# Second stage of a fused transformer kernel: who writes the rows of negated maxima

## The chip, the cores and the metric

The kernel runs on one core of one Trainium2 chip. The metric is the time on the device in microseconds; lower is better. Three runs of the kernel before took 1945.25, 1947.76 and 1950.1 us, so the median is 1947.76 us.

## The reference

The input x is (4, 256, 512) and the context is (4, 1601, 512), all in float32. Four blocks follow one another, each adding to x what it computes of layernorm(x):

```
x = x + L0_xattn(layernorm(x), ctx)   # latent cross attention, 16 heads, 1601 keys
x = x + L0_ffn(layernorm(x))          # int4 weights, dequantised by groups of 128
x = x + L1_xattn(layernorm(x), ctx)   # grouped attention, 16 heads on 4 key heads, 256 + 1601 keys
x = x + L1_ffn(layernorm(x))          # a dense layer plus a mixture of low-rank experts
```

The change is in the first block:

```
C_q = Q @ Wq_d;  C_kv = K @ Wkv_d
scores = einsum('bnhl,bkl->bhnk', (C_q @ W_qk).reshape(b, n, H, LKV), C_kv) / sqrt(LKV)
attn = softmax(scores, axis=-1)
out = einsum('bhnk,bkhd->bnhd', attn, (C_kv @ Wv_u).reshape(b, nkv, H, HD))
```

## The kernel before, in words

The kernel has three stages. The first turns the context and multiplies it with the key and value weights. The second (`latent_attention_and_ffn`) does the first attention and the dequantised layer. The third (`grouped_attention`) does the rest. Each engine runs its own list of instructions in a written order, and semaphores join them.

The second stage goes through 16 groups s (4 batches by 4 groups of 4 heads). A group has 1024 queries, which lie along the free axis, and 13 tiles of keys. For each tile TensorE multiplies keys with queries (`scores`, L952, two halves of 512 columns), ScalarE takes the exponential (L1080), and TensorE multiplies the result with the values (`values`, L965).

The softmax needs the maximum of every query before its scores are exponentiated. So a group's maxima are found one group ahead: TensorE computes 32 tiles of plain scores with the queries on the partitions (L1020), VectorE reduces each along the keys (L1187) and folds the 32 columns into `mx`, 128 x 8 (L1193). TensorE transposes `mx` into 8 rows of 128 in PSUM (L1023). From them `shift_rows` (L124) writes 8 rows of 1024 below the queries in `ast`: row j holds the negated maxima of its own 128 queries and zeros elsewhere, as a product of the 8 transposed rows, repeated eight times, with the small diagonal `negid`, repeated along its 128 columns. The keys have rows of ones beside them, so that the scores of L952 come out with the maximum subtracted. The product that makes the 8 rows of group s is called row s here; row 16 belongs to the third stage's first group and goes to `home[1]`.

All small products (maxima, rows, the raising of a finished group's output, queries, keys and values of the third stage) share a ring of four PSUM banks. Product n waits until product n - 4 has been read (`read`, L851). `course(s)` (L800) writes down the order of a group's work for all engines. Near its end stand: the values of tiles 10 and 11; row s + 1; three maxima of group s + 2; the values of tile 12; then the `tail`, which for groups 4 to 13 holds products of the other layers (an `ffn` pair, or one or two of `q`); then three more maxima. Then the next group's scores begin, and the first of them waits for `row_done` (L946). Groups 0 to 3, 14 and 15 have no tail.

GpSimd has little to do in this stage: a few memsets at its start, and nine times the inverse square root of a layernorm (`pool_root`, L87), each a chain of 14 small instructions, which starts when VectorE has the statistics and on which VectorE waits later.

Of the kernel before, what the change touches and what calls it, by code (L numbers as in the profile page):

```python
# [13 lines left out]
P = 128  # L14
BANK = 512
B, T, D = 4, 256, 512
# [7 lines left out]
H1, KV1, HD1 = 16, 4, 96  # L24
S1 = float(HD1) ** -0.5
G = 4
NG = H0 // G
GC = G * T
QT = GC // P
# [57 lines left out]
def pool_root(pool, chain, mv, v, t, y):  # L87

    chain.link(pool.tensor_scalar(v[:, :], mv[:, :, 1], EPS, None, ALU.add))  # L89
    chain.link(pool.tensor_scalar(y[:, :].bitcast(I32), v[:, :].bitcast(I32), -0.5, RSQRT_GUESS, ALU.mult, ALU.add))  # L90
    for i in range(3):
        chain.link(pool.tensor_tensor(t[:, :], y[:, :], y[:, :], ALU.mult))
        chain.link(pool.tensor_tensor(t[:, :], t[:, :], v[:, :], ALU.mult))
        chain.link(pool.tensor_scalar(t[:, :], t[:, :], -0.5, 1.5, ALU.mult, ALU.add))
        last = pool.tensor_tensor(y[:, :], y[:, :], t[:, :], ALU.mult)
        if i < 2:
            chain.link(last)
    return last
# [23 lines left out]
def shift_rows(dve, rows, turned, negid):  # L122

    return dve.tensor_tensor(rows.rearrange("p (j m) -> p j m", j=QT),  # L124
                             turned.rearrange("p (o m) -> p o m", o=1).broadcast_to([QT, QT, P]),
                             negid[:, :].rearrange("p (j o) -> p j o", o=1).broadcast_to([QT, QT, P]), ALU.mult)
# [562 lines left out]
def latent_attention_and_ffn(nc, A, ident, negid, ps, ln, home, wkvh, wkvl, wqh, wql, w0T, bias0, wqd, wqk, wvu, cq,  # L689
# [7 lines left out]
    S = B * NG  # L697
# [14 lines left out]
    with ExitStack() as ctx:  # L712
        def sb(name, shape, dt=F32):
            return ctx.enter_context(nc.sbuf_tensor(name, shape, dt))

        def sem(name):
            return ctx.enter_context(nc.semaphore(name))
# [9 lines left out]
        ast = sb("ast", [HD1 + QT, H0 * T], F32R)  # L727
        pr = sb("pr", [P, NPR, GC])
        osb = sb("osb", [P, BANK])
        pm = sb("pm", [P, QT, len(cuts)])  # L730
        mx = sb("mx", [P, QT])
        rec = sb("rec", [P, TT * G])
        tmp = sb("tmp", [P, TT, G * HD0])
        qst = sb("qst", [P, 2, 2, BANK])
# [4 lines left out]
        xa_done, xn_done = sem("xa_ready"), sem("xn_ready")  # L739
        k0_in, q0_in = [sem("k0_in0"), sem("k0_in1")], [sem("q0_in0"), sem("q0_in1")]  # L740
        ahi, xth_done, qhi = sem("a_hi"), sem("xt_hi"), sem("q_hi")
        mxr_done, row_done = sem("max_ready"), sem("max_row")
        s_mm, exp_done, av_mm, o_done = sem("scores"), sem("probs"), sem("values"), sem("o_copied")
        product = sem("ring_product")
        done = {"act": sem("ring_read_by_act"), "dve": sem("ring_read_by_dve")}
# [3 lines left out]
        stats_done, root_done = sem("norm_stats"), sem("norm_root")  # L749
# [83 lines left out]
        def last_reader(g):  # L833
            if g[0] in ("xat", "cq") or g[0] == "xt" and g[2:] == (0, 0):
                return "act"
            return "dve"

        at, order, count = {}, [], {"act": 0, "dve": 0}
# [5 lines left out]
        def bank_of(g):  # L844
            return bank(M0 + at[g][0] % RB)

        def turned(g):

            return product, at[g][0] + 1

        def read(g):  # L851

            return (row_done, g[1] + 1) if g[0] == "row" else (done[last_reader(g)], at[g][1])

        def qkv_free(e, u):

# [2 lines left out]
        def width(u):  # L859
            return WK if u >= NQ + NKL else T if u == NQ + NKL - 1 else 2 * T  # L860
# [65 lines left out]
        @block.gpsimd  # L926
        def _(pool):
            ready = Chain(pool, const, 0)
            for i in range(2):
                ready.link(pool.memset(cst[i][0:HD1, NC:NC + 1].bitcast(F32), 0.0))  # L930
            ready.link(pool.memset(home[0][0:HD1, NK:NK + 1].bitcast(F32), 0.0))
            ready.link(pool.memset(home[0][HD1:HD1 + QT, :].bitcast(F32), 1.0))
            ready.link(pool.memset(cst[1][HD1:HD1 + QT, :].bitcast(F32), 1.0))
            ready.link(pool.memset(cv[:, :, :, HD0:64], 0.0))
            ready.link(pool.memset(cv[:, :, :, HD0:HD0 + 1], 1.0))
            roots = Chain(pool, step_r, 0)
            for n in range(3 * (B - 1)):
                pool.wait_ge(stats_done, n + 1)
                pool_root(pool, roots, ln["mv"], ln["v"], ln["t"], ln["y"]).then_inc(root_done, 1)

        @block.tensor
        def _(pe):
# [56 lines left out]
            def ring_item(g):  # L999
                n, out = at[g][0], bank_of(g)  # L1000
                if n >= RB:
                    pe.wait_ge(*read(order[n - RB]))
# [121 lines left out]
        def _(dve):  # L1124
# [8 lines left out]
            norms, waiting = [0], []  # L1133
# [11 lines left out]
            def normalise_xa(f):  # L1145
                dve.wait_ge(xa_in, 16 * f)
                begin_norm(xa, xa, chain_a, xa_done)

            def normalise(e, k):
                if e < B - 1:  # L1150
                    begin_norm(x[:, e % 2, :, :], xn, chain, xn_done)
                else:
                    layernorm(dve, chain, xn, x[:, e % 2, :, :], ln["st"], ln["mv"], ln["v"], ln["t"], ln["u"], ln["y"])\
                        .then_inc(xn_done, 1)
# [22 lines left out]
            def ring_item(g):  # L1177
                if last_reader(g) == "act":
                    return
                src = bank_of(g)  # L1180
                if g[0] == "max":
                    _, s, i = g
                    if i == 0 and s:
                        dve.wait_ge(mxr_done, s)
                    dve.wait_ge(*turned(g))
                    j, ch = divmod(i, len(cuts))
                    dve.reduce_max(pm[:, j, ch:ch + 1], src[:, 0:(cuts if s < S else next_cuts)[ch][1]], AX)\  # L1187
                        .then_inc(done["dve"], 1)
                    if i == NI - 1:
                        dve.wait_ge(*read(g))  # L1190
                        if s:
                            dve.wait_ge(*turned(("row", s - 1)))
                        dve.reduce_max(mx[:, :], pm[:, :, :], AX).then_inc(mxr_done, 1)  # L1193
                elif g[0] == "row":
                    grp = g[1] % NG
                    dve.wait_ge(*turned(g))
                    rows = ast[HD1:HD1 + QT, grp * GC:(grp + 1) * GC] if g[1] < S \
                        else home[1][HD1:HD1 + QT, 0:GC]
                    shift_rows(dve, rows, src[0:QT, 0:P], negid).then_inc(row_done, 1)
                elif g[0] == "raise":  # L1200
                    dve.wait_ge(*turned(g))
                    attended(g[1], src)
                    b, grp = divmod(g[1], NG)
                    if grp == NG - 1:
                        normalise(b, 0)
                    if grp == 1 and b + 1 < B:
                        normalise_xa(b + 1)
                elif g[0] == "a":
                    lo = ast[2 * HD0:3 * HD0, g[2] * BANK:(g[2] + 1) * BANK]
                    dve.wait_ge(ahi, 8 * g[1] + g[2] + 1)  # L1210
                    dve.tensor_tensor(lo, src[2 * HD0:3 * HD0, :], lo, ALU.subtract).then_inc(done["dve"], 1)
                elif g[0] == "xt":
                    cols = slice(2 * g[3], 2 * g[3] + 2)
                    if g[2] == 0:
                        dve.wait_ge(*turned(g))
                        dve.tensor_copy(xT[:, cols, :], src.rearrange("p (c m) -> p c m", c=2)).then_inc(done["dve"], 1)
                    else:
                        dve.wait_ge(xth_done, 2 * g[1] + g[3] + 1)
                        dve.tensor_tensor(xtl[:, cols, :], src.rearrange("p (c m) -> p c m", c=2), xth[:, cols, :],
                                          ALU.subtract).then_inc(done["dve"], 1)  # L1220
                elif g[0] == "ffn":
                    _, e, t = g
                    xs = x[:, e % 2, t, :]
                    dve.wait_ge(*turned(g))
                    dve.tensor_tensor(xs, src, xs, ALU.add).then_inc(done["dve"], 1)
                    dve.wait_ge(*read(g))
                    chain.link(dve.tensor_tensor(xs, xs, bias0[:, :], ALU.add))
                    if t == TT - 1:
                        normalise(e, 1)
                else:  # L1230
                    _, e, u = g
                    n = width(u)
                    dve.wait_ge(qhi, NU * e + u + 1)
                    dve.tensor_tensor(qst[:, u % 2, 1, 0:n].bitcast(F32R), src[:, 0:n], qst[:, u % 2, 0, 0:n], ALU.subtract)\
                        .then_inc(done["dve"], 1)
# [663 lines left out]
```

## Time and profile before

| what | value |
|---|---|
| median of three runs | 1947.76 us |
| profiled execution, its own time | 1948.22 us |
| its span, first to last instruction | 1946.4 us |
| TensorE busy | 1872.9 us, 96% |
| VectorE busy | 1019.9 us, 52% |
| ScalarE busy | 904.3 us, 46% |
| GpSimd busy | 655.7 us, 34% |
| mean granted TensorE clock | 0.967 of full speed |

Times in the rows are from the start of the span. PE is TensorE's matrix multiplication, PEld its loading of weights (the left operand), which overlaps the multiplication before it; DVE is VectorE, ACT ScalarE, POOL GpSimd. A bracket shows how long the engine sat idle before the first instruction of the row and who released it. In a timeline, like instructions that follow each other are merged, with their count behind x.

### The profile page before, as it was taken

How to read it: one execution, taken by the hardware profiler on the slowest of the kernel's cores; microseconds unless marked ns; L12 is line 12 of the kernel's file. 1: busy time of each engine (PE TensorE's matmuls, PEld its weight loads, DVE VectorE, ACT ScalarE, POOL GpSimd, SP SyncE). 2: the span in 40 equal slices, each digit the busy share in tenths (PEclk: the TensorE clock that was granted, in tenths of full speed). 3: DMA queues.
4: the chain of work that ended last, by engine and by line, in shares of the span. 5: the costliest groups of instructions: out<-in, count | busy, mean ns of one | idle time of the engine just before them, and what ended most of it. 6: DMA issues, size and time to landing. Idle time of an engine off the chain costs nothing. (4 is left out here: it accounts for less than half of the span.)

```text
span 1946.4 us, 23155 instructions
## 1 busy us (share of the span) xinstructions
PE 1872.9 (96%) x8570; PEld 1337.1 (69%) x8570; DVE 1019.9 (52%) x1852; ACT 904.3 (46%) x1726; POOL 655.7 (34%) x630
## 2 busy tenths in 40 slices
PE   7999997999999999999979999999999999999998
PEld 6999894444465555555577777767777677777764
DVE  3464434667655565665635555554444645554415
ACT  2333331445334344444326666645666456655660
POOL 0000000000000000000017777755777577766770
PEclk9999996899999999999989999999999999999998
DMA  5978863000010111021058444544444355443201
GB/s 182 286 243 268 280 209 113 1 1 18 29 59 27 34 66 33 33 67 44 22 177 197 111 108 118 133 124 116 126 113 112 81 132 135 124 124 98 69 25 44
DMA packets 192950, 208.42 MB, mean 107 GB/s; under 512 B 87425, under 2 KB 157569, under 8 KB 192838
## 3 DMA queue, kind: packets, MB, share of 16 engines
q1 hardware_dynamic: 177124, 188.92, 34.1%
q10 hardware_dynamic: 15714, 18.03, 3.1%
q8 instruction: 68, 1.11, 0.2%
q14 instruction: 44, 0.36, 0.1%
HBM read 128.90 MB, written 77.94 MB: 106 GB/s over the span
## 5 line engine op out<-in xcount | busy, mean ns | idle before, releaser
L1475 POOL TENSOR_TENSOR pl<-pf,ph 128x512 fp32r<-128x512 f32 (+1 forms) x480 | 623.4, 1320 | 258.6 <-ACT pf L1669 258.6
L1666 ACT ACTIVATE ph<-ps 128x512 fp32r<-128x512 f32 (+1 forms) x480 | 288.4, 601 | 361.9 <-PE ps L1562 361.9
L1749 DVE TENSOR_REDUCE pm<-ps 128x1 f32<-128x464 f32 x480 | 307.7, 642 | 249.5 <-PE ps L1493 245.9
L1187 DVE TENSOR_REDUCE pm<-ps 128x1 f32<-128x400 f32 (+3 forms) x544 | 283.1, 572 | 96.9 <-PE ps L1020 84.0
L1080 ACT ACTIVATE pr<-ps 128x512 f32<-128x512 f32 (+1 forms) x416 | 219.1, 601 | 193.9 <-PE ps L952 192.9
L1669 ACT ACTIVATE pf<-ps 128x512 f32<-128x512 f32 (+1 forms) x480 | 289.7, 603 | 0.7 <-POOL pl L1475 0.7
L965 PE MATMUL ps<-pr,cv 128*64 128x512 f32 (+1 forms) x832 | 209.0, 618 | 0.0
L1580 PE MATMUL ps<-ph,vh 128*97 128x512 f32 (+1 forms) x480 | 193.0, 402 | 0.0
L1583 PE MATMUL ps<-pl,vh 128*97 128x512 f32 (+1 forms) x480 | 190.1, 396 | 0.8 <-POOL pl L1475 0.7
L1581 PE MATMUL ps<-ph,vl 128*97 128x512 f32 (+1 forms) x480 | 189.9, 396 | 0.0
L89 POOL TENSOR_SCALAR ln_v<-ln_mv 128x2 f32<-128x2 f32 x9 | 1.9, 214 | 507.1 <-DVE ln_mv L70 507.1
L1493 PE MATMUL ps<-kh,qh 96*128 96x464 f32 x320 | 121.3, 379 | 5.6 <-DVE pm L1749 5.6
L1560 PE MATMUL ps<-qh,kh 104*128 104x512 f32 x300 | 121.7, 406 | 0.0
L965 PEld LDWEIGHTS ps<-pr,cv 128*64 128x64 f32 (+1 forms) x832 | 51.9, 139 | 88.1 <-issue 59.9
L1583 PEld LDWEIGHTS ps<-pl,vh 128*97 128x97 f32 (+1 forms) x480 | 78.3, 163 | 36.0 <-POOL pl L1475 2.8
L930 POOL MEMSET home<- 96x1 f32 x1 | 0.1, 95 | 305.1 <-POOLq L186 305.1
L1581 PEld LDWEIGHTS ps<-ph,vl 128*97 128x97 f32 (+1 forms) x480 | 79.3, 165 | 27.1 <-issue 0.5
L1020 PE MATMUL ps<-home,ast 96*128 96x400 f32 (+1 forms) x256 | 91.1, 419 | 6.4 <-DVE pm L1187 3.2
L1580 PEld LDWEIGHTS ps<-ph,vh 128*97 128x97 f32 (+1 forms) x480 | 78.9, 164 | 25.1 <-issue 0.7
L1020 PEld LDWEIGHTS ps<-home,ast 96*128 96x128 f32 x256 | 50.3, 210 | 56.0 <-DVE pm L1187 25.8
L1020 PE MATMUL ps<-cst,ast 96*128 96x400 f32 (+1 forms) x256 | 83.1, 384 | 4.9 <-DVE pm L1187 3.5
L1020 PEld LDWEIGHTS ps<-cst,ast 96*128 96x128 f32 x256 | 46.0, 192 | 50.2 <-DVE pm L1187 28.2
(273 smaller groups left out, 3098.2 us busy)
## 6 DMA issues: line engine op xcount, KB each, us to landing
woT<-wo_turned SPq DMA_DIRECT2D x30, 768.0 KB, 6.1
v_scr<-vst SPq DMA_DIRECT2D x16, 1152.0 KB
cnat<-in_ctx_dram SPq DMA_DIRECT2D x16, 768.0 KB
q_scr<-qst SPq DMA_DIRECT2D x48, 256.0 KB, 2.5
vh<-v_scr SPq DMA_DIRECT2D x15, 672.0 KB
vl<-v_scr SPq DMA_DIRECT2D x15, 672.0 KB
home<-k_scr SPq DMA_DIRECT2D x14, 696.4 KB, 8.9
k_scr<-home SPq DMA_DIRECT2D x24, 384.0 KB, 7.8
```

What stands on the lines that cost most here:

```text
L965: mm = pe.matmul(bank(OB)[64 * half:64 * half + 64, :], cv[0:keys[kt], b % 2, kt, :], pr[0:keys[kt], n % NPR, half * BANK:(half + 1) * BAN ...
L1020: mm = pe.matmul(out[:, 0:k], queries, keys_t, start=True, stop=True)
L1080: act.activation(pr[0:keys[kt], n % NPR, half * BANK:(half + 1) * BANK], bank((2 * n + half) % SB)[0:keys[kt], :], ACT.Exp, scale=S0).then ...
L1187: dve.reduce_max(pm[:, j, ch:ch + 1], src[:, 0:(cuts if s < S else next_cuts)[ch][1]], AX)\
L1475: pool.tensor_tensor(pl[0:m, n % 2, cols], pf[0:m, half, :], ph[0:m, n % 2, cols].bitcast(F32), ALU.subtract).then_inc(plo, 1)
L1560: pe.matmul(out, kh[s % 3][:, k0:k0 + m], qh[s % 3][:, cols], start=True, stop=False)
L1580: pe.matmul(out, vh[0:m, s % 2, kt, :], ph[0:m, n % 2, cols], start=(kt == 0), stop=False)
L1581: pe.matmul(out, vl[0:m, s % 2, kt, :], ph[0:m, n % 2, cols], start=False, stop=False)
L1583: mm = pe.matmul(out, vh[0:m, s % 2, kt, :], pl[0:m, n % 2, cols], start=False, stop=(kt == KT - 1))
L1666: act.activation(ph[0:keys[kt], n % 2, cols], src, ACT.Exp, scale=S1).then_inc(phi, 1)
L1669: act.activation(pf[0:keys[kt], half, :], src, ACT.Exp, scale=S1).then_inc(exp_done, 1)
L1749: ins = dve.reduce_max(pm[:, j, ch:ch + 1], at[:, 0:cuts[ch][1]], AX)
```

## The change

The product of `shift_rows` moves from VectorE to GpSimd. GpSimd does not read PSUM in this kernel, so VectorE now copies the transposed 8 rows of 128 from PSUM into a new SBUF tile `turned_row`, and a new semaphore `row_read` tells of this copy. The ring's bank of a row is free with `row_read` and no longer with `row_done`. GpSimd waits for `row_read`, writes the 8 rows of 1024 and then raises `row_done`, on which the scores of the group wait as before. VectorE's copy waits for the `row_done` of the row before, since `turned_row` is a single buffer. GpSimd's program now goes through the groups, with the nine roots in between: for each group s a root first where one is due (at the first group of a batch but batch 0, and at the third group where another batch follows), then row s + 1, then the second root of a batch's first group.

```diff
@@ latent_attention_and_ffn
+        turned_row = sb("turned_row", [QT, P])
...
-        mxr_done, row_done = sem("max_ready"), sem("max_row")
+        mxr_done, row_read, row_done = sem("max_ready"), sem("max_row_read"), sem("max_row")
...
-            return (row_done, g[1] + 1) if g[0] == "row" else (done[last_reader(g)], at[g][1])
+            return (row_read, g[1] + 1) if g[0] == "row" else (done[last_reader(g)], at[g][1])
@@ gpsimd
-            for n in range(3 * (B - 1)):
-                pool.wait_ge(stats_done, n + 1)
+            norms, rows_given = [0], [0]
+
+            def root():
+                norms[0] += 1
+                pool.wait_ge(row_done, rows_given[0])
+                pool.wait_ge(stats_done, norms[0])
                 pool_root(pool, roots, ln["mv"], ln["v"], ln["t"], ln["y"]).then_inc(root_done, 1)
+
+            def row(s):
+                grp = s % NG
+                rows_given[0] += 1
+                if norms[0]:
+                    pool.wait_ge(root_done, norms[0])
+                pool.wait_ge(row_read, s + 1)
+                rows = ast[HD1:HD1 + QT, grp * GC:(grp + 1) * GC] if s < S else home[1][HD1:HD1 + QT, 0:GC]
+                shift_rows(pool, rows, turned_row[:, :], negid).then_inc(row_done, 1)
+
+            row(0)
+            for s in range(S):
+                b, g = divmod(s, NG)
+                if g == 0 and b or g == 2 and b + 1 < B:
+                    root()
+                row(s + 1)
+                if g == 0 and b:
+                    root()
@@ vector
                 elif g[0] == "row":
-                    grp = g[1] % NG
                     dve.wait_ge(*turned(g))
-                    rows = ast[HD1:HD1 + QT, grp * GC:(grp + 1) * GC] if g[1] < S \
-                        else home[1][HD1:HD1 + QT, 0:GC]
-                    shift_rows(dve, rows, src[0:QT, 0:P], negid).then_inc(row_done, 1)
+                    if g[1] > 0:
+                        dve.wait_ge(row_done, g[1] - 0)
+                    dve.tensor_copy(turned_row[:, :], src[0:QT, 0:P]).then_inc(row_read, 1)
```

## Rows read from the trace of the kernel before

**Rows 1.** The page's part 1: engine, busy us (share of the span), instructions.

```profile
PE 1872.9 (96%) x8570; PEld 1337.1 (69%) x8570; DVE 1019.9 (52%) x1852; ACT 904.3 (46%) x1726; POOL 655.7 (34%) x630
```

**Rows 2.** Busy time by stretch; the middle stretch is the second stage's groups.

```profile
345.00:951.00 606.00, 589.44 (x2664) 324.53 (x2662) 372.88 (x744) 261.84 (x499) 24.54 (x126) 0.98 0.11 33
```

**Rows 3.** The timeline at row 2: start us, us, engine line op, idle before.

```profile
402.31 0.49 PEld L1020 LDWEIGHTS ps<-home,ast 96*128 96x128 f32 x3
...
402.62 1.22 DVE L124 TENSOR_TENSOR ast<-ps,negid 8x1024 fp32r<-8x1024 f32 x1 [0.83 <-PE ps L1023]
...
403.06 0.20 PEld L965 LDWEIGHTS ps<-pr,cv 65*64 65x64 f32 x4 [0.26 <-issue]
...
403.87 3.94 DVE L1187 TENSOR_REDUCE pm<-ps 128x1 f32<-128x400 f32 x8
...
404.07 0.19 PEld L1020 LDWEIGHTS ps<-home,ast 96*128 96x128 f32 x1 [0.81 <-DVE ast L124]
...
405.08 0.37 PEld L952 LDWEIGHTS ps<-ast,home 104*128 104x128 f32 x2
...
405.75 2.06 ACT L1080 ACTIVATE pr<-ps 128x512 f32<-128x512 f32 x4 [0.97 <-PE ps L952]
...
406.40 0.19 PEld L952 LDWEIGHTS ps<-ast,home 104*128 104x128 f32 x1 [0.48 <-ACT pr L1080]
```

**Rows 4.** The timeline at row 0, before the first scores.

```profile
344.08 1.34 PE L1020 MATMUL ps<-home,ast 96*128 96x400 f32 x3
...
344.37 1.22 DVE L124 TENSOR_TENSOR ast<-ps,negid 8x1024 fp32r<-8x1024 f32 x1 [0.56 <-PE ps L1023]
...
346.89 0.67 PEld L952 LDWEIGHTS ps<-ast,home 104*128 104x128 f32 x2
```

**Rows 5.** The timeline at row 15.

```profile
919.30 0.51 PEld L1020 LDWEIGHTS ps<-home 96*128 96x128 f32 x3
...
919.61 1.22 DVE L124 TENSOR_TENSOR ast<-ps,negid 8x1024 fp32r<-8x1024 f32 x1 [0.83 <-PE ps L1023]
...
920.14 0.20 PEld L965 LDWEIGHTS ps<-pr,cv 65*64 65x64 f32 x4 [0.33 <-issue]
...
922.21 0.40 PEld L952 LDWEIGHTS ps<-ast,cst 104*128 104x128 f32 x2
```

**Rows 6.** The timeline at row 6, which has a product behind it.

```profile
550.64 1.22 DVE L124 TENSOR_TENSOR ast<-ps,negid 8x1024 fp32r<-8x1024 f32 x1 [0.84 <-PE ps L1023]
...
552.10 0.54 PEld L974 LDWEIGHTS ps<-xth,wqh 128*128 128x128 f32 x4 [0.81 <-DVE ast L124]
...
555.40 0.37 PEld L952 LDWEIGHTS ps<-ast,cst 104*128 104x128 f32 x2
```

**Rows 7.** Groups by form on GpSimd: busy us, mean ns, idle before.

```profile
L1475 POOL TENSOR_TENSOR pl<-pf,ph 128x512 fp32r<-128x512 f32 x448 | 582.9, 1322 | 251.9 <-ACT pf L1669 251.9
...
L93 POOL TENSOR_TENSOR ln_t<-ln_t,ln_v 128x2 f32<-128x2 f32 x27 | 5.3, 195 | 2.1
```

**Rows 8.** Groups by form on VectorE.

```profile
L650 DVE COPY cn<-ps 128x96 f32<-128x96 f32 x48 | 11.9, 248 | 0.0
...
L1767 DVE COPY dlall<-ps 128x8 f32<-128x8 f32 x4 | 0.7, 166 | 1.3 <-PE ps L1541 1.3
```

**Rows 9.** The timeline of VectorE and GpSimd around one layernorm root.

```profile
644.18 0.18 DVE L70 BATCH_NORM_AGGREGATE ln_mv<-ln_st 128x2 f32<-128x6 f32 x1
...
644.46 0.21 POOL L89 TENSOR_SCALAR ln_v<-ln_mv 128x2 f32<-128x2 f32 x1 [77.73 <-DVE ln_mv L70]
...
648.05 0.19 POOL L95 TENSOR_TENSOR ln_y<-ln_y,ln_t 128x2 f32<-128x2 f32 x1
...
648.28 0.57 DVE L1187 TENSOR_REDUCE pm<-ps 128x1 f32<-128x400 f32 x1 [2.49 <-POOL ln_y L95]
```

**Rows 10.** GpSimd's first TENSOR_TENSOR of the kernel, on the timeline.

```profile
412.42 0.19 POOL L90 TENSOR_SCALAR ln_y<-ln_v 128x2 int32<-128x2 int32 x1
...
412.70 0.19 POOL L92 TENSOR_TENSOR ln_t<-ln_y 128x2 f32<-128x2 f32 x1
```

## The prediction

> **What bounds the kernel now.** I read the busy times of the page first. TensorE is busy 1872.9 us of the span, VectorE and GpSimd far less [rows 1]. A view by stretches says the same of the second stage's groups: of 606 us, TensorE is busy 589.44, VectorE 372.88 and GpSimd 24.54 [rows 2]. So VectorE time given back is worth nothing by itself here; it counts only where TensorE waits for VectorE. The question is what happens to TensorE at the 17 places where a row is made, and this needs the timeline.
>
> At row 2, L124 starts on VectorE at 402.62 and takes 1.22 us, until 403.84. TensorE meanwhile loads weights for three maxima from 402.31 and for the values of the last tile from 403.06. It loads for the fourth maximum at 404.07 and for the next group's scores at 405.08, which is 2.46 us after the start of L124 [rows 3]. So `row_done` comes 1.24 us before TensorE would use it: there is slack, but not much. Rows 1, 3 and 4 stand in the same pattern, with distances of 2.47 us. Row 0 has 2.52 us (344.37 to 346.89) [rows 4], row 15 has 2.60 us (919.61 to 922.21) [rows 5]. The ten rows 5 to 14 have a tail between the row and the scores. Row 6 is one of the tightest of them, and there the distance is 4.76 us (550.64 to 555.40) [rows 6]. Row 16 is written before the last products of the stage and is not needed until the third stage.
>
> **What the change does to this path.** Let t be the moment at which L124 starts now; VectorE's copy will start there.
>
> The copy of 8 x 128 from PSUM: no such form is in the trace, but copies from PSUM of 96 and of 8 columns took 248 and 166 ns [rows 8], 0.93 ns for a column, so 128 columns take about 278 ns. VectorE is released 0.94 us earlier than now. Its additional wait, for the row before, was met a whole group ago, so nothing queues behind it.
>
> Handing over from VectorE to GpSimd: L70 ends at 644.36 and L89 starts at 644.46, 0.10 us. Handing over from GpSimd: L95 ends at 648.24 and VectorE starts at 648.28, 0.04 us [rows 9]; I take 0.05 towards TensorE, as L124's own release of TensorE is of that kind.
>
> GpSimd's product of 8 x 1024: this form is not in the trace. GpSimd's product-like instructions with two inputs took 1322 ns for 512 columns and 195 ns for 2 [rows 7]: 2.21 ns for a column, so 195 + 1022 x 2.21 = 2453 ns. Bounds: twice the 512-column instruction, 2.64 us, above, and below what VectorE takes for the very same form, 1.22 us [rows 3]. I take 2.45, since the form is nearest to L1475's: two float32 inputs, one output, only longer; whether 8 partitions or repeated operands change anything, no row shows.
>
> The Trainium skill ("GPSIMD Engine Reference", section 3.1) puts a two-input `tensor_tensor` on GpSimd at about 2.6 cycles an element, and 2048 elements at 4497 ns against 2293 on VectorE; scaled to 1024 elements that is an estimate of 2.25 us, by which each late row below would come 0.2 us earlier. The slope of [rows 7] is what this kernel's own instructions show, so the sum goes by that. The same page advises VectorE for elementwise work, as about twice as fast, which is the ratio between 2.45 and 1.22 here.
>
> So `row_done` reaches TensorE at t + 0.28 + 0.10 + 2.45 + 0.05 = t + 2.88, where it was at t + 1.24 or so. What was early becomes the last wait:
> - rows 1, 2, 3, 4: 2.88 instead of 2.46, 0.42 us late, four times: 1.68 us;
> - row 0: 2.88 instead of 2.52: 0.36 us;
> - row 15: 2.88 instead of 2.60: 0.28 us;
> - rows 5 to 14: 2.88 is before 4.76, nothing;
> - row 16: nothing.
>
> The sum is 2.3 us.
>
> Does a late start of the scores get lost further on? After it ScalarE sets the pace: its exponentials run back to back for four from 405.75, and TensorE's next load of scores, at 406.40, waits for one of them [rows 3]. That chain begins with the first scores, so it shifts whole. TensorE's work afterwards is what it was, so I count the delay in full.
>
> **What the change gives back.** The fourth to sixth maximum of each pass are held back now: TensorE loads for the fourth at 404.07 and for the scores at 405.08, 1.01 us, while the first three took 0.75 (402.31 to 403.06) [rows 3]. With VectorE free 0.94 us earlier TensorE can do them at its own pace and be at the scores 0.26 us sooner. But these scores then wait for `row_done` at t + 2.88, so this gain is hidden behind the new wait and is not subtracted. It becomes real only if GpSimd is faster than 2.0 us. The ring's bank, free at t + 0.28 instead of t + 1.22, gives no more: in the tail case TensorE loads for the product behind the values at 552.10 [rows 6], which is after the old L124 had ended (551.86) and while TensorE is still multiplying the values, so no multiplication stood still for it.
>
> The nine roots. A root is put ahead of a row on GpSimd in six groups, and row s + 1 cannot pass it. The root of this kind that starts at 644.46 is done at 648.24 [rows 9], 3.8 us later; its statistics come early in a group and the row only at its end, tens of us on: no wait. The second root of a batch's first group stands behind the row and waits for statistics that VectorE takes in the next group, and its 3.8 us are over long before that group's row. Also, GpSimd runs beside VectorE after the row, but what VectorE does then is a run of eight reductions (3.94 us) that read PSUM [rows 3].
>
> The Trainium skill ("SBUF — State Buffer", section "Who interferes with whom") says that a VectorE instruction with two SBUF inputs contends with a GpSimd instruction that reads SBUF, and that `tensor_reduce` never does. By it the eight reductions keep their time; no row here can show it before the change.
>
> So: 1948.22 us for the profiled execution (span 1946.4) becomes 1950.5. The median of the runs shown is 0.46 below that execution, so I predict 1950.1 us, 0.12% more. About 0.3%, 5.8 us, is what a measurement of this kernel can tell from no change; this falls within.
>
> **The rivals.**
> - *VectorE's relief wins.* GpSimd does the 8 x 1024 product in under 2.0 us, perhaps because only 8 partitions are used or because `negid` repeats. Then TensorE reaches the scores at its own pace: 0.26 us earlier four times (1.04), 0.22 at row 15 (three maxima 0.84 instead of 1.06 us), and up to 0.46 at row 0, where six maxima at 0.447 us each from 344.08 end at 346.76 while scores multiply from about 347.22 [rows 4, 5]. The sum is -1.7 us: 1946.5 on the profile's basis, 1946.1 on the median's. For it: the maxima are visibly held by VectorE. Against it: 195 ns plus anything near 2.2 ns a column. Chance 0.07.
> - *The repeated operands are slow on GpSimd, and the change costs a measurable time.* It decides from the point where GpSimd's product takes over 3.1 us: then the six late rows together cost 0.42 + 0.65 or more each, about 6 us. With 4.9 us, which is double my value, `row_done` reaches TensorE at t + 5.33: 2.87 us late four times, 2.81 and 2.73 at rows 0 and 15, and about 0.57 at five rows with a tail like row 6, together 20 us, 1968. For it: the operand repeats are the one thing that L1475 does not have. Against it: VectorE shows no price for them at 1.22 us for 1024 columns. Chance 0.06.
> - *The delay is absorbed.* The scores start 0.4 us late, but TensorE has slack in the first tiles while ScalarE paces it, and the lateness is made good there: 1948.2 on the profile's basis, 1947.8 on the median's. Against it: it is ScalarE itself that starts late. Chance 0.06.
> - *GpSimd's first product pays a start-up.* Row 0 would be its first TENSOR_TENSOR. A start-up of X us makes row 0 late by X on top of the 0.36, once, and decides from 3.5 us on. Against it: the present first one, at 412.70, starts 0.09 us after the end of the instruction before it [rows 10]. Chance 0.01. The Trainium skill ("GPSIMD Engine Reference", section 2.1) gives about 6 us for the first call of freshly loaded code; by it the time would be 1956, and the trace shows no such gap.
>
> **How the numbers follow.** My forecast (GpSimd between 2.2 and 2.9 us) has 0.80 and holds from +0.8 to +5 us. The median itself moves: the three runs shown lie 2.5 us to either side. With the bounds of GpSimd's time, 2.64 us giving +3.4 and the case below 2.0 us giving -1.7, the range is 1946.3 to 1953.8. Slower than 0.3% needs the second or fourth rival: 0.07. Faster than 0.3% would need three times what the first rival gives: 0.02. Within: 0.91.
>
> **What would show it.** In the profile of the changed kernel: 17 TENSOR_TENSOR on GpSimd of about 2.45 us; 17 copies on VectorE of about 0.28; at rows 1 to 4 the load for the first scores waits for GpSimd and comes 2.9 us after the copy's start, after about 0.7 us in which TensorE has nothing; at rows 5 to 14 no such wait. I am wrong if the product takes under 2.0 or over 3.1 us, if TensorE waits at a row that has a tail, or if the second stage's groups don't get longer by 2 to 3 us.

## The result, and the profile after

The changed kernel takes 1943.78 us in the median of 20 runs (1940.33 to 1948.01); the kernel before takes 1948.24 us in 20 runs beside it (1942.53 to 1952.18). The ratio is 0.9981 with a 95% interval of 0.9974 to 0.9988: 3.7 us faster, 2.3 to 5.1. The forecast was 1950.1 us, 2.3 us slower, with a range from 1946.3 to 1953.8. So the sign is wrong and the time lies below the range.

The profiled execution took 1942.78 us, its span 1941.0. Engines and the second stage's groups, from the page's part 1 and the view by stretches (busy time of PE, PEld, DVE, ACT, POOL, then granted clock, DMA share, GB/s):

```profile
PE 1867.7 (96%) x8570; PEld 1334.6 (69%) x8570; DVE 1004.3 (52%) x1852; ACT 904.2 (47%) x1726; POOL 687.9 (35%) x647
```
```profile
344.00:945.00 601.00, 585.84 (x2662) 324.21 (x2662) 357.92 (x743) 261.31 (x498) 54.78 (x142) 0.98 0.11 33
```

VectorE has 15.6 us less than in [rows 1] and GpSimd 32.2 more, as the 17 moved rows want. The stretch between rows 0 and 16 went from 604.94 us (343.96 to 948.90) to 601.20 (343.23 to 944.43). The two moved instructions, as groups by form on GpSimd and on VectorE:

```profile
L124 POOL TENSOR_TENSOR ast<-turned_row,negid 8x1024 fp32r<-8x1024 f32 x16 | 30.3, 1891 | 452.4 <-DVE turned_row L1221 452.4
```
```profile
L1221 DVE COPY turned_row<-ps 8x128 f32<-8x128 f32 x17 | 4.7, 279 | 11.5 <-PE ps L1046 11.5
```

The copy takes 279 ns, as forecast. GpSimd's product takes 1891 ns, where 2453 were forecast.

The timeline at row 2, which answers to [rows 3]:

```profile
401.14 0.49 PEld L1043 LDWEIGHTS ps<-home,ast 96*128 96x128 f32 x3
...
401.45 0.28 DVE L1221 COPY turned_row<-ps 8x128 f32<-8x128 f32 x1 [0.83 <-PE ps L1046]
401.70 1.54 DVE L1210 TENSOR_REDUCE pm<-ps 128x1 f32<-128x400 f32 x3
401.80 1.89 POOL L124 TENSOR_TENSOR ast<-turned_row,negid 8x1024 fp32r<-8x1024 f32 x1 [26.78 <-DVE turned_row L1221]
401.89 0.20 PEld L988 LDWEIGHTS ps<-pr,cv 65*64 65x64 f32 x4 [0.26 <-issue]
...
402.90 0.48 PEld L1043 LDWEIGHTS ps<-home,ast 96*128 96x128 f32 x3 [0.81 <-issue]
...
403.75 0.30 PEld L975 LDWEIGHTS ps<-ast,home 104*128 104x128 f32 x2 [0.36 <-POOL ast L124]
...
404.35 2.06 ACT L1103 ACTIVATE pr<-ps 128x512 f32<-128x512 f32 x4 [0.74 <-PE ps L975]
...
404.99 0.19 PEld L975 LDWEIGHTS ps<-ast,home 104*128 104x128 f32 x1 [0.49 <-ACT pr L1103]
```

The copy starts at t = 401.45. GpSimd starts 0.07 us after the copy's end and is done at 403.69; TensorE's load of weights for the scores starts at 403.75, that is t + 2.30, and had waited 0.36 us for GpSimd. Before it was t + 2.46. The last three maxima are now loaded in one run from 402.90, with no wait for VectorE between them. ScalarE's chain follows as before.

The load is not the multiplication. On the timeline of TensorE's multiplications alone, before (t = 402.62) and after (t = 401.45):

```profile
405.26 0.62 PE L952 MATMUL ps<-ast,home 104*128 104x512 f32 x2
...
405.90 0.99 PE L952 MATMUL ps<-ast,home 104*128 104x512 f32 x2
```
```profile
402.90 0.82 PE L1043 MATMUL ps<-home,ast 96*128 96x402 f32 x3
403.75 0.73 PE L975 MATMUL ps<-ast,home 104*128 104x512 f32 x2
...
404.50 0.99 PE L975 MATMUL ps<-ast,home 104*128 104x512 f32 x2
```

Before, the load ran 0.18 us ahead of its multiplication; now both start together, so the first scores are multiplied 0.34 us earlier (t + 2.30 for t + 2.64), though the load gained only 0.16. The second pair of scores comes at t + 3.05 for t + 3.28, which is 0.23 us earlier: about 0.1 us of the gain is lost again between the first and the second pair. TensorE itself hardly stands still for GpSimd here: by the trace it multiplies maxima until 403.72.

Row 0 and row 15 on the timeline, which answer to [rows 4] and [rows 5]:

```profile
343.64 0.28 DVE L1221 COPY turned_row<-ps 8x128 f32<-8x128 f32 x1 [0.56 <-PE ps L1046]
344.07 1.89 POOL L124 TENSOR_TENSOR ast<-turned_row,negid 8x1024 fp32r<-8x1024 f32 x1 [31.80 <-DVE turned_row L1221]
...
346.01 0.50 PEld L975 LDWEIGHTS ps<-ast,home 104*128 104x128 f32 x2 [0.49 <-POOL ast L124]
```
```profile
915.48 0.28 DVE L1221 COPY turned_row<-ps 8x128 f32<-8x128 f32 x1 [0.83 <-PE ps L1046]
...
915.90 1.89 POOL L124 TENSOR_TENSOR ast<-turned_row,negid 8x1024 fp32r<-8x1024 f32 x1 [34.09 <-DVE turned_row L1221]
...
917.84 0.30 PEld L975 LDWEIGHTS ps<-ast,cst 104*128 104x128 f32 x2 [0.31 <-POOL ast L124]
```

There the load is at t + 2.37 (before 2.52) and t + 2.36 (before 2.60); the copy reaches GpSimd after 0.15 and 0.14 us, not 0.07. Rows 1, 3 and 4 have t + 2.30, 2.36 and 2.37 (before 2.47 each). At row 6, which answers to [rows 6], the scores are loaded at t + 4.76, exactly as before, and nothing waits for GpSimd:

```profile
547.85 0.28 DVE L1221 COPY turned_row<-ps 8x128 f32<-8x128 f32 x1 [0.84 <-PE ps L1046]
...
548.27 1.89 POOL L124 TENSOR_TENSOR ast<-turned_row,negid 8x1024 fp32r<-8x1024 f32 x1 [29.36 <-DVE turned_row L1221]
...
549.30 0.54 PEld L997 LDWEIGHTS ps<-xth,wqh 128*128 128x128 f32 x4 [0.81 <-issue]
...
552.61 0.37 PEld L975 LDWEIGHTS ps<-ast,cst 104*128 104x128 f32 x2
```

### The profile page after: what moved, and what is told of

Read it like the earlier page. It is cut to its first block and busy times, and to the rows that moved or that the text cites. A ratio compares the mean times of both kernels' runs of the same rounds, so it can differ in the third digit from the quotient of the medians.

```text
span 1941.0 us, 23211 instructions
## 1 busy us (share of the span) xinstructions
PE 1867.7 (96%) x8570; PEld 1334.6 (69%) x8570; DVE 1004.3 (52%) x1852; ACT 904.2 (47%) x1726; POOL 687.9 (35%) x647
## 5 line engine op out<-in xcount | busy, mean ns | idle before, releaser
L124 POOL TENSOR_TENSOR ast<-turned_row,negid 8x1024 fp32r<-8x1024 f32 x16 | 30.3, 1891 | 452.4 <-DVE turned_row L1221 452.4
L975 PE MATMUL ps<-ast,home 104*128 104x512 f32 (+1 forms) x208 | 77.2, 432 | 1.9
```

## The distances between the rows

The transposition of `mx` on TensorE is one and the same instruction in all kernels, so the distance from one row to the next compares group with group. The first column is the changed kernel's first profile minus that of the kernel before; the others are profiles of the experiments below (us, minus is shorter):

| from row to row | changed | rows_no_tail | rows_tail | row_padded | second profile of before |
|---|---|---|---|---|---|
| 0 to 1 | -0.19 | -0.18 | -0.36 | +0.21 | +0.12 |
| 1 to 2 | -0.26 | -0.25 | -0.01 | +0.26 | -0.01 |
| 2 to 3 | -0.24 | -0.24 | +1.60 | +1.91 | +0.03 |
| 3 to 4 | -0.16 | -0.16 | +0.02 | +0.35 | 0.00 |
| 4 to 5 | -1.68 | -1.68 | -1.58 | -1.15 | +0.01 |
| 5 to 6 | +0.47 | +0.48 | +0.51 | +0.47 | 0.00 |
| 6 to 7, 7 to 8 | 0.00 | -0.03, 0.00 | -0.03, -0.01 | -0.02, +0.03 | -0.02, -0.01 |
| 8 to 9 | -1.53 | -1.52 | -1.51 | -1.49 | +0.02 |
| 9 to 15 | +0.18 | +0.20 | +0.22 | +1.70 | +0.11 |
| 15 to 16 | -0.33 | -0.34 | 0.00 | +0.18 | -0.01 |

The first line is weak evidence. From row 0 to row 1 the five profiles of before, listed further below, differ by 0.50 us among themselves (-0.38 to +0.12 against the first) and those of the changed kernel by 1.33 (-0.66 to +0.67), with the same mean, about -0.1. The small differences at 1 to 2, 2 to 3, 3 to 4 and 15 to 16 come back in every profile of the changed kernel, once the stretches named next are set aside.

Two kinds of difference stand side by side: small ones of 0.1 to 0.35 us behind the rows without a tail, and large ones of about 1.6. Of the -1.68 from 4 to 5, 1.58 is of the large kind and about 0.10 of the small. The large ones are stretches in which TensorE's granted clock is at 1.2 GHz, and not 2.4. They stand behind the root of the layernorm: VectorE stands still for GpSimd, TensorE runs out of products, and in some executions its clock falls. The +0.47 from 5 to 6 is of the same origin and not an effect of the change: groups 5, 9 and 13 have a stretch of half clock in all ten profiles of the two kernels, and its length varies. From row 5 to row 6 the mean granted clock is 0.96 in the first profile of before, and 0.93 in the changed kernel's; it is 0.93 also in the fifth profile of before, where this distance is 0.49 longer. The view by stretches in group 4 of the kernel before (the column before the last two is the granted clock):

```profile
479.72:482.72 3.00, 2.11 (x9) 0.47 (x5) 1.42 (x3) 0.34 (x1) 1.10 (x6) 1.00 0.00 0
482.72:485.72 3.00, 2.70 (x10) 1.91 (x11) 3.00 (x7) 1.53 (x3) 0.00 (x0) 0.83 0.00 0
485.72:488.72 3.00, 3.00 (x10) 0.76 (x9) 0.62 (x2) 1.14 (x3) 0.00 (x0) 0.60 0.00 0
```

and of the changed kernel at the same distance from its row 4:

```profile
478.14:481.14 3.00, 1.95 (x9) 0.47 (x5) 1.51 (x3) 0.17 (x1) 1.01 (x6) 1.00 0.00 0
481.14:484.14 3.00, 2.80 (x13) 1.74 (x15) 3.00 (x8) 1.82 (x4) 0.00 (x0) 1.00 0.00 0
484.14:487.14 3.00, 3.00 (x16) 1.34 (x13) 1.12 (x3) 0.84 (x2) 0.00 (x0) 1.00 0.00 0
```

In both TensorE is busy for about 2 of 3 us at the stall; only the first has the half clock after it.

## Experiments

**One part of the change alone, and the change again.** `rows_no_tail` and `rows_tail` keep the copy and GpSimd's product for some rows and write the others with VectorE from PSUM as before:

```diff
+        def by_pool(s):
+            return s < 5 or s > 14          # rows_tail: 5 <= s <= 14
...
-                    dve.tensor_copy(turned_row[:, :], src[0:QT, 0:P]).then_inc(row_read, 1)
+                    if by_pool(g[1]):
+                        dve.tensor_copy(turned_row[:, :], src[0:QT, 0:P]).then_inc(row_read, 1)
+                    else:
...
+                        shift_rows(dve, rows, src[0:QT, 0:P], negid).then_inc(row_done, 1)
```

> Rows 0 to 4, 15 and 16 are written by GpSimd from the copy, rows 5 to 14 by VectorE from PSUM as before. Theory A (the path): GpSimd's product takes 1.89 us, so row_done comes before TensorE would want it, and the three maxima behind it are no longer held by VectorE; that gain of 0.2 to 0.3 us lies at the rows without a tail alone. This kernel then has all of it: 1.2 to 1.7 us less than before. Theory B (the clock): what the changed kernel gained beyond that is that stretches of half clock after the root of groups 4 and 8, 1.5 to 1.7 us each, come in fewer executions; they are set off by TensorE's stall there, and whether they come in an execution depends on its moment and not on who writes the rows. By it the profile of this kernel may show or lack either stretch. Theory C (VectorE's time): the whole of the gain comes from VectorE's 0.94 us at all 17 rows; then this kernel has less than half of the changed kernel's gain.

> Rows 5 to 14 are written by GpSimd from the copy, the others by VectorE from PSUM as before. Theory A: no gain at all from the path, the distance from the copy to the next scores there is over 4.7 us; 0 us, give or take the clock's stretches. Theory C: more than half of the changed kernel's gain, 2 us or more.

> The changed kernel itself, a second profile and times on the same chip as the others. All theories: about 0.998 of before. Theory B: at groups 0 to 3 and 14 the same gains of 0.16 to 0.33 us as in its first profile; in groups 4, 8 and 12 the stretches of half clock may come again.

Measured, beside the same runs of the kernel before: rows_no_tail 0.9984 (0.9975 to 0.9993), rows_tail 1.000 (0.999 to 1.0011), after_again (unchanged from the changed kernel) 0.9984 (0.9975 to 0.9992). By the medians the whole gain is with the seven rows 0 to 4, 15 and 16. The ten rows with a tail bring nothing that shows, though VectorE is relieved at each of them: the interval of rows_tail leaves room for 2 us, but its distances behind rows 5 to 14 are those of before, but for the stretches of half clock. Theory C falls. The timeline of rows_tail at row 2, where VectorE still writes the row, has the old 2.46 us:

```profile
401.30 1.22 DVE L124 TENSOR_TENSOR ast<-ps,negid 8x1024 fp32r<-8x1024 f32 x1 [0.83 <-PE ps L1057]
...
403.76 0.37 PEld L986 LDWEIGHTS ps<-ast,home 104*128 104x128 f32 x2
```

**The forecast's own duration.** `row_padded` is the changed kernel with a small product ahead of each row:

```diff
+                pads.link(pool.tensor_tensor(spare[:, :], spare[:, :], spare[:, :], ALU.mult))   # 8 x 160
                 shift_rows(pool, rows, turned_row[:, :], negid).then_inc(row_done, 1)
```

> The changed kernel with a product of 8 x 160 on a spare tile ahead of each row on GpSimd, after its wait, so that the row comes 0.5 to 0.6 us later, as if the product took the 2.45 us that was forecast. Theory A (the sum of the forecast was right but for GpSimd's product): row_done now reaches TensorE 2.85 to 2.9 us after the copy's start, rows 0 to 4 and 15 are late by 0.3 to 0.4 us against before, and the kernel loses 3 to 4 us against the changed one; against before it is 0 to 2.5 us slower. Rival: the lateness is made good behind ScalarE, and the kernel stays where the changed one is, 0.998.

Measured: 1.0011 (1.0002 to 1.0019), 2.1 us slower than before, as expected. Against the changed kernel (0.9984 in after_again) that is some 5 us, more than the 3 to 4 that I expected. Its timeline at row 2: the product now ends 2.41 us after GpSimd's first instruction has started, and the load for the scores comes at t + 2.82, held by GpSimd for 0.89 us.

```profile
402.19 0.28 DVE L1225 COPY turned_row<-ps 8x128 f32<-8x128 f32 x1 [0.83 <-PE ps L1050]
...
402.55 0.45 POOL L956 TENSOR_TENSOR spare<-spare 8x160 f32<-8x160 f32 x1 [26.78 <-DVE turned_row L1225]
...
403.07 1.89 POOL L124 TENSOR_TENSOR ast<-turned_row,negid 8x1024 fp32r<-8x1024 f32 x1
...
405.01 0.30 PEld L979 LDWEIGHTS ps<-ast,home 104*128 104x128 f32 x2 [0.89 <-POOL ast L124]
```

TensorE's multiplication now does wait, for 0.55 us. The column of the table gives 0.21, 0.26, 0.35 and 0.18 us of lateness against before. With the stretches of half clock taken out (1.6 us more in 2 to 3, 1.58 less in 4 to 5) it gives about 0.3 and 0.43 as well: 1.7 us in all. The forecast's sum for a path of 2.82 is 6 x 0.06 less than 2.32, 2.0 us. So the sum was nearly right in this direction; its one badly wrong term was the product. Between this kernel and the changed one the rows' path gives 1.7 + 1.3 = 3.0 us of the 5.

**What a product costs on GpSimd.** `probe_forms` adds to the changed kernel, in groups 9 and 11, eight products of 384 columns:

```diff
+                for p in (P, QT):
+                    probes.link(pool.tensor_tensor(pb_[0:p, :], pa[0:p, :], pb_[0:p, :], ALU.mult))
+                    probes.link(pool.tensor_tensor(cut(pb_, p), cut(pa, p), along(p), ALU.mult))
+                    probes.link(pool.tensor_tensor(cut(pb_, p), again(p), cut(pb_, p), ALU.mult))
+                    probes.link(pool.tensor_tensor(cut(pb_, p), again(p), along(p), ALU.mult))
```

`along` repeats one value over 128 columns, as `negid` in the row; `again` repeats 128 columns three times, as the copied row.

> The changed kernel, and in groups 9 and 11, behind the row, eight products of 384 columns on GpSimd: on 128 and on 8 partitions, each with two plain operands, with one repeated along the columns (as negid), with one repeated as a whole (as the copied row), and with both. The forecast took 2.21 ns a column for all; the row's own 1890 ns say 1.66. If the repeat along the columns is what is cheap, the forms with it take 0.83 us and the others 1.04; if it is the 8 partitions, all of those take 0.83 and none of the 128; if it is only the two together, only both on 8.

Measured (groups by form; L956 has two plain operands, L957 `along`, L958 `again`, L959 both):

```profile
L956 POOL TENSOR_TENSOR pb_<-pa,pb_ 128x384 f32<-128x384 f32 x2 | 2.0, 1016 | 0.2
L958 POOL TENSOR_TENSOR pb_<-pa,pb_ 128x384 f32<-128x384 f32 x2 | 2.0, 1012 | 0.2
L956 POOL TENSOR_TENSOR pb_<-pa,pb_ 8x384 f32<-8x384 f32 x2 | 2.0, 998 | 0.2
L958 POOL TENSOR_TENSOR pb_<-pa,pb_ 8x384 f32<-8x384 f32 x2 | 2.0, 994 | 0.2
...
L959 POOL TENSOR_TENSOR pb_<-pa,ident 8x384 f32<-8x384 f32 x2 | 1.8, 886 | 0.2
...
L957 POOL TENSOR_TENSOR pb_<-pa,ident 128x384 f32<-128x384 f32 x2 | 1.7, 827 | 0.2
L959 POOL TENSOR_TENSOR pb_<-pa,ident 128x384 f32<-128x384 f32 x2 | 1.7, 826 | 0.2
...
L957 POOL TENSOR_TENSOR pb_<-pa,ident 8x384 f32<-8x384 f32 x2 | 1.6, 817 | 0.2
```

The operand that repeats one value over its columns makes the product cheap, 827 ns in place of 1016 on 128 partitions. With the 195 ns of a tiny product in [rows 7] taken off both, that is 1.65 and 2.15 ns a column, and 195 + 1022 x 1.65 = 1881 ns for the row, against 1891 measured. The repeat as a whole changes nothing (1012), and 8 partitions cost nearly what 128 do (998 beside 1016). Each form ran only twice. The two runs of the form with both repeats on 8 partitions took 817 and 956 ns, so that its mean is 886; why one was slower is not known. By the Trainium skill ("GPSIMD Engine Reference", section 3.1) the cost of a two-input product is that of fetching two elements in turn through one port; the plain forms agree with its 2.6 cycles an element, which at the page's 1.2 GHz is an estimate of 2.17 ns, while the form with `along` costs less than it says.

**Where the half clock falls.**

> The kernel before itself, for a second profile and the granted clock of each execution. Ratio 1.000. Theory B (the clock's stretches fall at other moments in each execution): the two stretches of half clock that its first profile has in groups 4 and 8 need not come again there; the distances between rows differ by 1.6 us from the first profile where one comes or goes, and by under 0.05 elsewhere. Rival: they come in groups 4 and 8 each time with the rows on VectorE, so that they are an effect of who writes the rows.

> The kernel before, a third profile. Theory B: the second stage from row 0 to row 16 takes 603.5 us plus 1.6 for each stretch of half clock behind a root in groups 2, 4, 8 and 12 (none would leave 602); the two seen so far had two each. The rival that who writes the rows decides it: again in groups 4 and 8, 605.0 us.

> The changed kernel, a third profile. From row 0 to row 16: 601.2 us without a stretch of half clock behind a root, 602.9 with one (seen so far: none, and one in group 12).

> The kernel before, a fourth profile. If its stretches of half clock lie where they lay three times, groups 4 and 8 and 605.1 us from row 0 to row 16; if they fall by chance, another number.

> The changed kernel, a fourth profile. 601.2 us from row 0 to row 16 and 1.7 for each stretch behind a root; if it has as many as the kernel before this would be 2, and by the gain still unexplained it is 1 on the mean.

> The kernel before, a fifth profile, expected as the fourth: two stretches, 605.1 us from row 0 to row 16.

> The changed kernel, a fifth profile, expected as the fourth: one stretch on the mean of all, 601.2 us and 1.7 for each.

All are the two kernels themselves, and a p in the name stands for one profiled execution. before_again, with 11 runs, has a ratio of 0.9997 (0.9987 to 1.0007). The profiles, with the first ones:

| kernel | rows 0 to 16, us | groups with half clock behind the root |
|---|---|---|
| before, five profiles | 604.94, 605.18, 605.14, 605.92, 603.46 | 4, 8; 4, 8; 4, 8; 2, 8, 12; 2 |
| changed, five profiles | 601.20, 602.96, 604.66, 602.77, 601.92 | none; 12; 8, 12; 12; 4 |

In the table the groups counted are 2, 4, 8 and 12. Not all of my expectations held: after_p3 had two stretches and 604.66 us where I named at most one, before_p4 had three, before_p5 one, and after_p5, with one, was 1.0 us below the 602.9 of its sum. The first three profiles of before spoke for the rival that writing the rows on VectorE puts the stretches into groups 4 and 8; the fourth and fifth refute it, as does rows_tail, which has its one stretch in group 2 (rows 0 to 4 are VectorE's there). The view by stretches of group 2 in the first profile and in the fourth, one and the same kernel:

```profile
416.00:419.00 3.00, 1.94 (x7) 0.97 (x6) 2.96 (x7) 0.57 (x2) 0.00 (x0) 1.00 0.01 3
419.00:422.00 3.00, 3.00 (x17) 1.29 (x15) 1.94 (x5) 1.97 (x5) 0.00 (x0) 1.00 0.00 0
```

```profile
412.50:415.50 3.00, 1.93 (x7) 0.96 (x6) 2.96 (x7) 0.54 (x2) 0.00 (x0) 1.00 0.01 3
415.50:418.50 3.00, 3.00 (x12) 1.71 (x12) 2.05 (x5) 2.07 (x5) 0.00 (x0) 0.58 0.00 0
418.50:421.50 3.00, 3.00 (x15) 1.50 (x12) 0.47 (x1) 0.66 (x2) 0.00 (x0) 0.85 0.00 0
```

The same stall, 1.94 and 1.93 us busy of 3, is followed by full clock once and by 0.58 the other time. The Trainium skill ("TensorE: Matmul & The Clock Gate", Part 1) says that what watches TensorE's activity runs free of the kernel, so that the same kernel differs between runs; these two stretches agree with that.

On the mean before has 2.0 stretches and 604.93 us, the changed kernel 1.0 and 602.70: 2.2 us apart. Of these up to 1.3 are the rows' path; the rest is the balance of the stretches, one of 1.6 us fewer in groups 2, 4, 8 and 12 against somewhat longer ones in groups 5, 9 and 13. The mean granted clock of the core was 0.9684, 0.9688, 0.9691 and 0.9688 in four sets of runs of before (29, 21, 9 and 11), and 0.9701 and 0.9703 in two of the changed kernel (20 and 11). That points the same way, but row_padded has 0.9699 and is slower than before, and rows_tail has 0.9696 and is no faster. Why the changed kernel should have fewer stretches is not shown. Five profiles of each don't exclude chance, and two kernels that differ from the changed one only by small products on GpSimd, row_padded and probe_forms, had two stretches each in their one profile.

These distances hold only the second stage. Up to row 0 the ten profiles of the two kernels take 340.5 to 345.5 us, and behind row 16 995.9 to 998.9. Over the whole span the five profiles of before have a mean of 1944.8 us and those of the changed kernel 1944.5, so that they don't even show the gain that the timed runs do; what a single profile says of the whole time is worth little here.

**Moving the wait for the root.** `norm_later_before` and `norm_later_after` have one edit to the kernel before and to the changed one:

```diff
-                waiting.append([4, norms[0], x_rows, out, chain_of, ready])
+                waiting.append([7, norms[0], x_rows, out, chain_of, ready])
```

VectorE turns to the normalised rows after seven of its products and not four, and by then the root is nearer its end.

> The kernel before, with one edit: VectorE turns to the end of a layernorm seven products after its statistics and not four, so that it does not stand still for GpSimd's root. Theory B: the stall of TensorE after the root (about 1 us in each of groups 4, 8 and 12) goes, and with it the half-clock stretches in those groups: 3 us from the stalls and up to 3 us from the clock, 3 to 6 us less than before. A rival: the stall moves to the transposes that wait for the normalised rows, or TensorE made it good later anyway; then 0 to 1 us.

> The changed kernel and VectorE's end of a layernorm after seven products and not four. Theories A and B add up: the 1.3 to 1.7 us of the rows and the gain of the later end, which alone was a ratio of 0.9947: 0.993 to 0.9945. Rival: the two overlap, and it is 0.9947 or more.

> The kernel before with the later end of the layernorms (seven products), timed beside the next one. In its first timing it was a ratio of 0.9947 with few executions; the same is expected.

> The changed kernel with the later end of the layernorms. With TensorE's stalls behind the roots gone, Theory B says that what the changed kernel gains beyond the rows' 1.3 us has nothing to come from: this kernel is 1 to 1.7 us faster than the one beside it. Rival (the extra comes from somewhere else than the stalls behind the roots): it is 3 to 4 us faster, as the changed kernel is against the one before.

| kernel | ratio to before | rows 0 to 16, us |
|---|---|---|
| norm_later_before | 0.9947 (0.9928 to 0.9965) | 594.82 |
| nl_before_2, the same | 0.9948 (0.9936 to 0.9961) | 594.43 |
| norm_later_after | 0.9936 (0.9922 to 0.9950) | 596.12 |
| nl_after_2, the same | 0.9938 (0.9925 to 0.9952) | 594.49 |

Waits of VectorE for the roots in the second stage (total us, times, longest) in the kernel before, and in norm_later_before:

```profile
DVE pm L1187 <- POOL ln_y L95: 10.1, 4, 2.6
...
DVE rec L1162 <- POOL ln_y L95: 7.5, 3, 2.5
```

```profile
DVE pm L1187 <- POOL ln_y L95: 4.3, 6, 1.1
```

17.6 us of waiting became 4.3, and none of the four profiles has half clock behind a root in groups 2, 4, 8 or 12. TensorE's stall is smaller but not gone. In group 4 two waits for VectorE before, of 0.51 and 0.62 us, became one of 0.93 for the normalised rows (TensorE's multiplications alone, before and norm_later_before):

```profile
481.90 0.45 PE L1020 MATMUL ps<-cst,ast 96*128 96x400 f32 x1 [0.51 <-DVE pm L1187]
482.96 0.45 PE L1020 MATMUL ps<-cst,ast 96*128 96x400 f32 x1 [0.62 <-DVE pm L1187]
```
```profile
480.98 0.63 PE L995 MATMUL ps<-ident,xn 128*128 128x128 f32 x4 [0.93 <-DVE xn L106]
```

So the expectation's rival had a part of it right. Whether the half clock stays away because the stall is shorter, or because it lies elsewhere, these runs don't show. This edit alone is worth 10 us, more than the 3 to 6 that I gave it. I had named groups 4, 8 and 12; in the first profile the distances behind rows 2, 5, 9 and 13 are shorter too, by 0.87, 1.17, 0.92 and 1.25 us. With the change it is 12, the best of all kernels tried. By the ratios the change adds 0.0011 and 0.0010 to it, about 2 us; timed side by side, the medians of nl_before_2 and nl_after_2 are 1936.85 and 1936.41. Theory B said 1 to 1.7, its rival 3 to 4; the intervals are too wide to exclude the latter, so this only leans to Theory B. In the second stage the profiles show no gain of the change (596.12 and 594.49 against 594.82 and 594.43). The distances 1 to 2, 2 to 3, 3 to 4 and 15 to 16 are shorter by the same 0.16 to 0.34 us, and the varying half clock in groups 5, 9 and 13 outweighs them.

## Why the prediction was wrong, point by point

- *TensorE bounds the stage, and only the wait at the rows counts.* Right: the tail rows bring nothing (rows_tail, 1.000), at row 6 the distance stayed 4.76 us.
- *The copy, the two handovers.* Right: 279 ns for 278. VectorE's end reaches GpSimd after 0.07 us at row 2 and 0.14 to 0.15 at rows 0, 6 and 15, for 0.10; GpSimd's reaches TensorE after 0.06 for 0.05.
- *A start-up of GpSimd's first product.* Not seen: row 0's starts 0.15 us after the copy and takes 1.89 us like the others.
- *GpSimd's product, 2.45 us.* This step failed: 1.89. I took the slope of L1475 for a form with a repeated operand and wrote that no row shows whether the repeat matters; the probe shows that it does. At 1.89 the term is under the 2.0 us at which the forecast itself put the change of sign, and the forecast's own path becomes t + 2.32, where t + 2.30 to 2.37 was measured.
- *What was early becomes the last wait.* The load's wait for GpSimd is there at rows 0 to 4 and 15, but it ends 0.10 to 0.24 us before the old start and not 0.28 to 0.42 later. The first rival, VectorE's relief, is what happened; it had 0.07. Its 1.7 us compare with 1.28 in the distances: 0.19, 0.26, 0.24, 0.16, 0.10 and 0.33, where 0.10 is 1.68 less the 1.58 that rows_tail shows for the stretch alone. The 0.19 of row 0 lies within that distance's scatter, so what repeats is 1.1 us. At row 2 the rival's 0.26 is nearly reached (0.24); rows 3, 4 and 0 stay below their shares, and row 15 has 0.33 for 0.22.
- *The delay counts in full.* Nearly: row_padded has 1.7 us of lateness for the 2.0 of the sum. I measured it at the load; the first multiplication came 0.18 us behind the load before, and in the changed kernel starts with it.
- *The range.* Its lower end, 1946.3, is about what the case below 2.0 us gives (1946.1), with nothing for the median's own movement; its upper end is +3.4 and 2.5 us for that movement. With 2.5 us on both sides it would have begun near 1943.6. The rows give at most 1.3 us of a measured 3.7 (2.3 to 5.1): with the right product the forecast would have had the sign and less than half of the size. I had no term for TensorE's clock, although about 1.6 us hang on each stall behind a root that is followed by the half clock or not.

What stays open: the rows' path is shown for 1.1 to 1.3 us. That the rest comes from fewer stretches of half clock is argued from five profiles of each kernel and could be chance in them; with it the second stage comes to 2.2 us, a little below the measured interval. Where the remainder is, no experiment shows. Rows_no_tail and row_padded do show that it goes with the seven rows: it is there when they are early (0.9984), and gone when they are late (1.0011).

## What to carry to other kernels

When work is moved to a slower engine off the critical path, what decides is the distance at which its result is awaited, place by place: find it on the timeline, at the multiplication as well as at the load of its weights, and find the duration at which the sign changes. If the estimate lies within a third of that duration, the chance belongs on both sides, and the form with its repeats has to be priced, not the operation's name. And look at the stalls first: turning to the roots' results three products later, where VectorE had waited up to 2.6 us at a time, was worth nearly three times the whole change.

## What the runs showed of the hardware

A two-input product on GpSimd cost 1.65 ns a column in probe_forms, above a base of 195 ns, when one operand repeated a single value over the columns, and 2.15 when it did not, on 8 partitions nearly as on 128. A stall of TensorE of about 1 us in 3 was followed in some executions by a stretch at 1.2 GHz that cost 1.6 us, and in others, of the same kernel, by none: in the five profiles of before, 10 of the 20 stalls behind the roots of groups 2, 4, 8 and 12.
